# Two elementwise multiplies of a quantised feed-forward stage move from VectorE to GpSimd

## The reference

```
x = layernorm(x + attn_ref(x))          # stage A, written to memory in bf16
h = bitlinear(x, norm1_w, w1)           # 1024 -> 4096
h = act_scale * relu(h)**2 + act_bias
y = bitlinear(h, norm2_w, w2)           # 4096 -> 1024
x = layernorm(x + y)

bitlinear(x, norm_w, w):
    x_norm = x * rsqrt(mean(x*x) + 1e-8) * norm_w
    scale  = 127 / max(|x_norm|)        # per token
    x_q    = clip(round(x_norm*scale), -128, 127) / scale
    w_q    = clip(round(w/mean|w|), -1, 1) * mean|w|
    return x_q @ w_q.T
```

## Time and profile before

| | us |
|---|---|
| median of 3 executions | 3213.95 (3208.13 to 3216.69) |
| profiled execution | 3213.92 |
| its span on the slowest core (core 2) | 3212.4 |
| DVE busy | 1620.2 (50%) |
| PE busy | 1410.7 (44%) |
| ACT busy | 786.8 (24%) |
| POOL busy | 71.4 (2%) |

### The profile page before, as it was taken

The page is one execution under the profiler, slowest core; times in us unless marked ns, Lnnn a source line. Parts: engine busy times, 40 slices in busy tenths (PEclk is TensorE's granted clock), DMA queues, the critical chain, the costliest instruction groups (busy, mean ns, idle before and its releaser), DMA issues.

```text
span 3212.4 us, 19690 instructions; the slowest of 8 cores (3194.2 to 3212.4 us)
## 1 busy us (share of the span) xinstructions
PE 1410.7 (44%) x4188; PEld 433.5 (13%) x4270; DVE 1620.2 (50%) x1691; ACT 786.8 (24%) x1164; POOL 71.4 (2%) x128
## 2 busy tenths in 40 slices
PE   0766566666566400000135443455344455334453
PEld 0122122222122100000011111111111111111110
DVE  2224334343434345553037766666666666666665
ACT  0010111111110100000034444444434444444442
POOL 0000000000000011100000000000000000000000
PEclk9877777778777655555566666666656666666665
DMA  3400000000000156778600000001000010000011
GB/s 83 158 13 0 10 20 11 20 10 20 10 20 4 36 177 199 254 242 231 129 7 18 23 23 23 21 20 23 23 22 22 17 25 22 22 23 22 17 23 27
DMA packets 203439, 166.46 MB, mean 52 GB/s; under 512 B 173625, under 2 KB 178490, under 8 KB 199227
## 3 DMA queue, kind: packets, MB, share of 16 engines
q1 hardware_dynamic: 186716, 82.34, 10.0%
q0 software_dynamic: 16608, 82.85, 8.4%
HBM read 100.09 MB, written 29.36 MB: 40 GB/s over the span
## 4 chain that ended last, share of the span: by engine, by line
DVE 39%; issue 13%; PEldq 13%; DMA 12%; ACT 9%; SPq 8%; PEld 3%; DVEq 2%; ACTq 1%; POOLq 0%
PEldq L175 13%; DVE g2s L882 12%; DMA wqf<-w 7%; DVE Pb L656 5%; SPq L1009 5%; ACT d2s L875 2%; DVE f2s L872 2%; DVE xq2o L888 2%; SPq L837 2%; DVE d2s L885 1%; DMA xq2Tc<-xq2o 1%; SPq L830 1%; DVE wqb L804 1%; DVEq L175 1%; DVE st_mu L510 1%
## 5 line engine op out<-in xcount | busy, mean ns | idle before, releaser
L1018 PE MATMUL yc<-wq2T,xq2Tc 128*128 128x512 bf16 x1004 | 403.8, 514 | 378.3 <-DMA xq2Tc<-xq2o 364.0
L980 PE MATMUL pj<-wq1T,xq1T 128*128 128x512 bf16 x1003 | 317.4, 445 | 485.8 <-DMA xq1T<-xq 416.8
L882 DVE SCALAR_TENSOR_TENSOR g2s<-d2s,g2s 128x1024 bf16<-128x1024 bf16 x368 | 450.8, 1225 | 45.5 <-issue 2.3
L1018 PEld LDWEIGHTS yc<-wq2T,xq2Tc 128*128 128x128 bf16 x1024 | 113.7, 115 | 659.5 <-issue 640.5
L980 PEld LDWEIGHTS pj<-wq1T,xq1T 128*128 128x128 bf16 x1024 | 99.7, 106 | 713.0 <-issue 650.7
L1038 DVE TENSOR_TENSOR t2f<-t2f,nw2r 128x1024 f32<-128x1024 f32 x64 | 78.4, 1225 | 149.5 <-ACTq L175 141.2
L934 ACT ACTIVATE t<-xp 128x1024 f32<-128x1024 bf16 x16 | 16.9, 1056 | 557.0 <-PEq L175 483.4
L875 ACT ACTIVATE d2s<-f2s 128x1024 bf16<-128x1024 bf16 x64 | 67.6, 1056 | 302.0 <-DVEq L175 302.0
L598 PE MATMUL pj<-Wg,xnT 128*128 128x512 bf16 x279 | 108.4, 553 | 75.4 <-DVEq L175 74.6
L598 PE MATMUL yc<-Wg,xnT 128*128 128x512 bf16 x562 | 135.5, 380 | 3.6 <-issue 0.2
L665 PE MATMUL pj<-Pb,s_winv 128*128 128x512 bf16 x193 | 96.0, 566 | 89.0 <-DVEq L175 88.5
(11 more groups left out here) (181 smaller groups left out, 2018.5 us busy)
## 6 DMA issues: line engine op xcount, KB each, us to landing
wqf<-w POOLq DMA_DIRECT2D x64, 512.0 KB, 4.0
wqf<-w POOLq DMA_DIRECT2D x16, 2048.0 KB, 12.2
wf<-W_in SPq DMA_DIRECT2D x8, 1536.0 KB, 6.7
xr<-x_own POOLq DMA_DIRECT2D x16, 512.0 KB, 4.0
sc_wq<-wqb SPq DMA_DIRECT2D x32, 256.0 KB, 2.2
sc_wq<-wqb SPq DMA_DIRECT2D x8, 1024.0 KB, 4.5
xq2Tc<-xq2o SPq DMA_TRANSPOSE x512, 2.3
out<-outb SPq DMA_DIRECT2D x16, 512.0 KB, 2.8
```

The source lines that it names most:

```text
L882: tn = sch.op("vector", (lambda lv: lambda e: e.scalar_tensor_tensor(gbuf[:, 0:width], dbuf[:, 0:width], 0.5 + lv, gbuf[:, 0:width], OP.is ...
L980: (lambda ss, dc, h: lambda e: e.matmul(pshalf("pj", h), xq1T[:, dc * 128:(dc + 1) * 128], wq1T[dc][:, ss * 1024 + h * 512: ss * 1024 + (h ...
L1018: (lambda k, q, oc, kb: lambda e: e.matmul(pshalf("yc1", oc), xq2Tc[kb][:, q * 128:(q + 1) * 128], wq2Tc[k * 8 + q][:, oc * 512:(oc + 1) * ...
```

## The change

Two `sch.op` calls name another engine and another semaphore: the multiply of L938 (one for each of 16 tiles, 128x1024, f32 from two bf16 operands) and the multiply of L1038 (four for each tile, 128x1024, f32 from f32 and bf16, in place) are recorded for GpSimd with semaphore Q. The operands, the tile sizes and the place in the Python code are the same. DVE's maximum behind each of them now waits for Q, where it followed in DVE's own queue.

```
-        tt1 = sch.op("vector", (lambda xpb: lambda e: e.tensor_tensor(
+        tt1 = sch.op("gpsimd", (lambda xpb: lambda e: e.tensor_tensor(
             t1[:], xp_t[xpb][:], nw1r[:], OP.mult))(xpb),
-            (tss, tok_xpl, tok_nw1r), "V")
+            (tss, tok_xpl, tok_nw1r), "Q")
...
-        tt2 = sch.op("vector", (lambda k: lambda e: e.tensor_tensor(
+        tt2 = sch.op("gpsimd", (lambda k: lambda e: e.tensor_tensor(
             t2f[:, k * 1024:(k + 1) * 1024],
             t2f[:, k * 1024:(k + 1) * 1024],
             nw2r[:, k * 1024:(k + 1) * 1024], OP.mult))(k),
-            (tss2, tok_nw2r if t == 0 else None), "V")
+            (tss2, tok_nw2r if t == 0 else None), "Q")
```

## The result

| | before | after |
|---|---|---|
| median of 8 executions, us | 3213.3 (3207.26 to 3217.03) | 3272.9 (3265.57 to 3279.03) |
| ratio | 1 | 1.0187 (95% interval 1.0173 to 1.0201) |
| span of the slowest core, us | 3212.4 | 3275.4 |

The change makes the kernel 59.6 us slower, 24 us less than the 84 us that were forecast. The time lies between the forecast (3298 us) and the first rival (3264 us), and by the number alone nearer to the rival (9 us against 25); the iterations of 101.4 us, too, are nearer to its 100.8 than to the forecast's 103. Which of the two mechanisms it is has to be read from the rows.

The account below looks back on a forecast made before the run. Two chains from DVE's roundings, ending nearly together at L1093, were taken to bound the iteration; 4.35 us there plus 1.2 at L938 made 5.55, 83 for 15, so 3213.9 + 84 = 3298 us; own range 3286 to 3307, wide 3225 to 3330.

Parts of the forecast that it names:

- the first rival: In stage B, POOL waits until DVE stops at L1043, roundings uninterrupted: 3.25 us an iteration, 3264 us; chance 0.25.
- the heavy POOL: POOL holds DVE and takes 3 us a multiply, overhead added to two passes: 8.35 us an iteration, 3340 us; chance 0.09.
- Holding: Beside the roundings, POOL waits for DVE's running instruction, then the next DVE instructions wait 2.3 us for POOL.
- The rival that DVE keeps its turn: Same as the first rival: POOL gets its turn only when DVE stops at L1043; 3264 us, chance 0.25.
- D: Estimated duration of one multiply on POOL: 2.3 us, the middle of the upper pair 2.1 and 2.45.
- chain A: Second rounding's end, transposes, matmuls, fourth superstrip, ACT, fourth multiply, small chain to L1093: forecast 4.45 us later.
- the forecast's 5.55 us: Forecast loss per iteration: L1093 about 4.35 us later plus 1.2 for L938; 83 us for 15.
- the 4.35 us in the sum: Forecast delay of L1093 in each iteration, with both chains taken to end together.
- Chain B: Third rounding's end, its eight transposes and PE's last matmuls to L1093: 0.25 us behind before, forecast 4.2 us later.
- Exchange: A covered multiply leaves DVE's queue, saving 1.35 us, but holds the rounding 2.3: 0.95 us later each.
- No contention: POOL works beside DVE unhindered, at 2.3 us a multiply: +0.8 us an iteration, 3226 us; chance 0.13.
- its quick variant: POOL unhindered and as quick as DVE, 1.225 us a multiply: gain of 1.4 us an iteration, 3193 us; chance 0.06.

Follow-up runs that it names:

- e1: Kernel before with only the L938 multiply moved to GpSimd, the four of L1038 staying on VectorE: ratio 1.0050.
- e2: Kernel before with only the fourth L1038 multiply of each tile moved to GpSimd: ratio 1.0063.
- e9: Kernel before plus one unused GpSimd multiply per tile, released by the fourth L1038 so that it meets the maximum L1043: ratio 1.0000.
- e5: Changed kernel with GpSimd's first three multiplies waiting until the rounding beside them has ended: ratio 1.0132 to the kernel before.
- e3: Kernel before with only the third L1038 multiply of each tile moved to GpSimd: ratio 1.0054.
- e10: Kernel before plus one unused 1024-column GpSimd multiply per rounding of a hidden piece (64), meeting the five L882: ratio 1.0252.
- e4: Kernel before with only the first L1038 multiply of each tile moved to GpSimd: ratio 1.0008.

## Why the prediction was right, and where its sizes were off

- **What was right and what was not.** The direction, the cause and the way of it came as forecast. The size did not: 3272.9 us lie outside the forecast's own range of 3286 to 3307, and inside the wide one of 3225 to 3330 because that was drawn around the rivals too.
- **The bound** was read right. Idle POOL was no gain, since 2 of the 5 multiplies stood uncovered (e1, e2: 0.99 and 0.88 us for each iteration) and 3 beside roundings.
- **The duration on POOL**, estimated at 2.3 us, was 2.12 (2.11 for L938), at the lower of the two upper bounds, which also excludes the heavy POOL of 3 us. The sum has it four times for each iteration: 4 x 0.19 = 0.76 us too much.
- **Holding**, taken over from one DMA issue and a one-operand DVE form, is right for L882, L885 and L888 (all 45 covered multiplies hold one of them), and POOL does get in between two of them. That it was taken "as general" on one row was luck in part: beside the maximum L1043 nothing is held on either side (e9), and all of these multiplies happened to meet two-operand instructions. The rival that DVE keeps its turn is excluded by the row of L885 (1784 ns), and its order (e5) has a ratio of 1.0132 against the change's 1.0187.
- **What DVE loses by being held** is the term that was sized wrong. I put the whole duration, "the next ones (L885, L888) wait D = 2.3 us"; DVE loses the duration less 0.47 us. That part sits twice in chain A (one exchange, one multiply ahead of the second rounding's end), 0.94 us an iteration too much.
- Both together, 0.76 + 0.94, take the forecast's 5.55 us to 3.85; measured are 3.87. That they meet to 0.02 is partly luck, since the 4.35 us in the sum do not follow from its own terms: with A 4.45 later, and B 4.2 later but 0.25 behind at the start, both chains end at the same time, 4.2 behind the old start of L1093. By segment: X0 to X2 3.25 forecast, 1.97 measured; the fourth multiply 1.2 and 0.85 to 0.97; L938 1.2 and 1.02.
- **Chain B**: I read from L1093's waits that B ended 0.25 us behind A. Waits count only the iterations in which B was last. On average B ended 0.6 us ahead of A (e3). It changed little in the sum, because A decides in most iterations of the changed kernel (L1093 starts 1.39 us behind PE's last matmul on average), but it put e3 and e10 too high.
- **Exchange**: +0.95 for one exchange on DVE was forecast; e4 shows 0.28.
- **No contention** and its quick variant are excluded by e3 (no loss was to be had there) and by POOL's 2.12 us.

## What to carry to other kernels

Before moving an elementwise step to an idle GpSimd, sort its instances: one that a waiting VectorE runs alone gets the full difference of the two engines on the path (0.97 us for 128x1024 here), and one that overlaps two-operand VectorE work costs VectorE more than it saves (1.65 against 1.35 us) and also moves the cost forward, to whatever is running when the step becomes ready. What looked like a load to take off an engine was a question of order on that engine: the same multiplies, with their maxima, behind the last rounding instead of between the roundings, gave 1.5%, and with one superstrip ahead of the transposes 2%. And two chains that end together need their slack read in both directions, since a row of waits shows only the iterations in which one of them is late.

## What the runs showed of the hardware that I had not expected

- The loss of a held VectorE instruction is GpSimd's duration less 0.40 us (1.89 and 1.49 us; half the columns, 1.04 and 0.64) or less 0.47 us (2.12 and 1.65 us). The rows show what the 0.40 and the 0.47 are made of.
- GpSimd's multiply ends its own duration less 0.14 us behind the end of the VectorE instruction that was running: 1.98, 1.75 and 0.90 us for 2.12, 1.89 and 1.04. The held VectorE instruction then ends its own duration less 0.14 us behind GpSimd's end: 0.55 for L885's 0.69, 1.08 for the 1.22 of L882. The loss is the multiply's duration less twice 0.14 and less the gap that stood in front of the held instruction anyway, 0.19 us ahead of L885 and 0.12 ahead of the second L882. So 0.40 or 0.47 is a matter of which instruction is held, not of the multiply's operands. A multiply of the changed kernel, of an f32 and a bf16 operand and 2.12 us long, that came late enough to hold L888 (gap 0.12) cost it 2.94 - 1.22 = 1.72 us, 0.40 less than 2.12:

```profile
2361.64 0.69 DVE L885 TENSOR_TENSOR d2s<-f2s,g2s 128x1024 bf16<-128x1024 bf16 x1 [0.19 <-ACTq L175]
2362.45 2.94 DVE L888 TENSOR_TENSOR xq2o<-it2s,d2s 128x1024 bf16<-128x1024 int32 x1
```

```profile
2361.65 2.65 POOL L1038 TENSOR_TENSOR t2f<-t2f,nw2r 128x1024 f32<-128x1024 f32 x1 [13.45 <-ACTq L175]
```

- The wait is booked in the durations: L885 reads 2.34 us and GpSimd's multiply 2.86, so VectorE looks busy while it is held. The idle columns show nothing of it (0.19 us as before); only the mean of a known form gives it away.
- GpSimd's multiply of two bf16 views of one tile takes 1.89 us, of two different bf16 tiles 2.11, and of an f32 and a bf16 tile 2.12. Whether the 0.2 us are the second tile's was not tried.
